# In the first three pairs POOL makes one of the eight broadcast additions of the attention scores

## What is computed

```python
x = emb[tokens] * jnp.sqrt(jnp.float32(D_MODEL))
x = x + positional_encoding(N, D_MODEL)[None, :, :]
q = x @ Wq + bq
k = x @ Wk + bk
v = x @ Wv + bv
scores = jnp.einsum('d,bijd->bij', attn_scale, jnp.tanh(q[:, :, None, :] + k[:, None, :, :]))
weights = jax.nn.softmax(scores, axis=-1)
attn = jnp.einsum('bij,bjd->bid', weights, v)
attn = attn @ Wo + bo
x = layer_norm(x + attn, g1, beta1)
h = jax.nn.relu(x @ W1 + bf1)
y = h @ W2 + bf2
return layer_norm(x + y, g2, beta2)
```

## Time and profile before

| | us |
|---|---|
| median of 3 runs | 890.82 |
| lowest and highest | 890.13, 891.63 |
| the profiled execution | 891.35 |
| its span, first to last instruction | 889.5 |
| busy, of the span: PE, DVE, ACT, POOL | 788.0, 659.6, 656.9, 324.7 |
| mean granted clock of TensorE (share of full) | 0.956 |

### The profile page before, as it was taken

How to read it: one execution, slowest core, us unless ns; L and a number is a source line. 1 busy time by engine, 2 the same in 40 slices (tenths; PEclk the granted TensorE clock), 3 DMA queues, 4 the chain that set the end, 5 groups by cost and what they waited for, 6 DMA issues and landing times. The chain is left out here.

```text
span 889.5 us, 22649 instructions
## 1 busy us (share of the span) xinstructions
PE 788.0 (89%) x7286; PEld 607.1 (68%) x7286; DVE 659.6 (74%) x2165; ACT 656.9 (74%) x1498; POOL 324.7 (36%) x397
## 2 busy tenths in 40 slices
PE   0857998998989989899899999987889999999798
PEld 0534665765766656667656666664779999999687
DVE  2997899999999999999999999553423344443675
ACT  1775999999898988998999999765335565655444
POOL 3110124334343353343433523444414545555121
PEclk9978999999999999999999999997889999999899
DMA  8129889889899889898898898894089999995411
GB/s 163 49 55 210 189 191 208 193 188 212 188 204 206 183 180 206 181 204 187 182 210 176 187 206 181 196 208 102 21 279 387 376 395 403 324 360 191 149 30 36
DMA packets 82305, 177.77 MB, mean 200 GB/s; under 512 B 8244, under 2 KB 35339, under 8 KB 82240
## 3 DMA queue, kind: packets, MB, share of 16 engines
q1 hardware_dynamic: 65536, 164.01, 73.9%
q0 software_dynamic: 5760, 7.92, 2.7%
q10 hardware_dynamic: 10944, 5.02, 2.1%
HBM read 65.93 MB, written 113.34 MB: 202 GB/s over the span
## 5 line engine op out<-in xcount | busy, mean ns | idle before, releaser
L879 DVE TENSOR_TENSOR arena<-qT,b_qk 128x2304 f32<-128x2304 f32 x128 | 323.8, 2543 | 1.6 <-DVE v_bias L904 0.3
L615 ACT ACTIVATE arena<-arena 128x2304 f32<-128x2304 f32 x128 | 271.6, 2122 | 41.8 <-DVE arena L879 40.9
L1324 PE MATMUL b_s<-arena,apad 128*32 128x192 f32 x3072 | 160.4, 345 | 30.9 <-ACT p L624 24.2
L760 ACT ACTIVATE act_h<-big,arena 128x128 f32<-128x128 f32 x336 | 96.1, 369 | 74.1 <-PE big L1641 69.7
L1324 PEld LDWEIGHTS b_s<-arena,apad 128*32 128x32 f32 x3072 | 90.5, 113 | 87.8 <-issue 43.0
L541 POOL TENSOR_TENSOR kept<-kept,rs 96x384 f32<-96x384 f32 x64 | 52.7, 824 | 215.0 <-DVE rs L1026 214.8
L589 POOL DMA_INDIRECT eo_dram<-gT,toff x84 | 82.5, 983 | 96.3 <-issue 64.3
L658 ACT ACTIVATE kept<-kept,mx 96x96 f32<-96x96 f32 x256 | 92.3, 365 | 11.9 <-DVE mx L1019 11.3
L1641 PE MATMUL big<-hbT,arena 128*128 128x128 f32 x672 | 91.2, 280 | 2.3 <-DVE hbT L1207 1.2
L1641 PEld LDWEIGHTS big<-hbT,arena 128*128 128x128 f32 x672 | 83.6, 196 | 3.1 <-issue 2.1
L1207 DVE TENSOR_SCALAR hbT<-b_t,cols 128x128 f32<-128x128 f32 x84 | 34.4, 409 | 65.0 <-PE b_t L1634 65.0
(11 more groups left out here) (209 smaller groups left out, 1441.4 us busy)
## 6 DMA issues: line engine op xcount, KB each, us to landing
rows_dram<-act_h SPq DMA_DIRECT2D x32, 3096.0 KB
arena<-in_wpack SPq DMA_DIRECT2D x84, 578.0 KB
prT<-rows_dram ACTq DMA_DIRECT2D x76, 64.5 KB
arena<-eo_dram SPq DMA_DIRECT2D x4, 512.0 KB, 6.9
x_dram<-res SPq DMA_DIRECT2D x16, 96.0 KB
out<-of SPq DMA_DIRECT2D x12, 128.0 KB, 1.8
eo_dram<-gT,toff POOLq DMA_INDIRECT x84
rows_dram<-rows_now,slot_now POOLq DMA_INDIRECT x64
```

The lines of the kernel that those rows point to most:

```text
L615: act.activation(v, v, ACT.Tanh).then_inc(s["tanh"], 1)
L760: last = act.activation(act_h[:, i, c * TILE:(c + 1) * TILE], big[i][:, c * TILE:(c + 1) * TILE], ACT.Silu, bias=wslot[:, slot, 2 * DFF + ...
L879: dve.tensor_tensor(ring[c % TRING].rearrange("p (x m n) -> p x m n", m=CQ, n=N), qv.unsqueeze(3).to_broadcast([D, SPLIT * QG, CQ, N]), kv ...
L1324: last = pe.matmul(b_s[32 * a:32 * a + 32, 0:SPLIT * N], apad[:, 31 - line:63 - line], t[:, :, a, m, :], start=(line == 0), stop=(line == ...
```

## The change

A helper `adds(p, c)` counts VectorE's additions up to chunk c of pair p, since the first three pairs have seven of them. In pairs 0, 1 and 2 (HELPED = 3) `qk_evac` first copies the keys from PSUM to a new SBUF tile kT; chunk 4 (HELD) is left out of VectorE's list and is made by POOL in `help_add`, from kT, which stands in POOL's list between root h0 and normalise 3. `help_add` waits for the queries of the pair and for score 0 of it. ScalarE's tanh 4 waits for POOL's semaphore `add_pool`. The waits on the semaphore `add` are counted anew. From pair 3 on, the list of instructions is as before, except for one wait on `add_pool` in pair 3.

```diff
@@ -52,6 +52,7 @@
 CH = G * CPB
 CW = SPLIT * QG * CQ * N
 TRING = 4
+HELPED, HELD = 3, 4
 EARLY = 2
 DEPTH = 5
 VC = D + 2
@@ -64,6 +65,13 @@
 WCOLS = 2 * DFF + FC + D
 
 ROWS = ["bo", "g2", "beta2", "bs2", "fbf2"]
+
+
+def adds(p, c):
+
+    if known(p) and p < HELPED:
+        return p * (CH - 1) + c - (c > HELD)
+    return p * CH + (c - HELPED)
 
 
 def known(value):
@@ -183,6 +191,7 @@
         xs = sb("xs", [N, G, D])
         xT = sb("xT", [D, TN])
         qT = sb("qT", [D, TN])
+        kT = sb("kT", [D, TN])
         bqk = sb("bqk", [D, 1])
         vrow = sb("vrow", [N, G, VC])
         nmax = sb("nmax", [128, SPLIT])
@@ -280,7 +289,7 @@
 
         s = {n: ctx.enter_context(nc.semaphore("s_" + n)) for n in [
             "ids", "ld_a", "ld_b", "late", "consts", "gate", "pool_c", "setup_mm", "setup",
-            "raw_mm", "raw_ev", "emb0", "emb1", "emb2", "eid", "xs", "kept", "xs_t", "xT", "qk", "qk_ev", "add", "tanh", "score",
+            "raw_mm", "raw_ev", "emb0", "emb1", "emb2", "eid", "xs", "kept", "xs_t", "xT", "qk", "qk_ev", "add", "add_pool", "tanh", "score",
             "nmax", "exp1", "p1t", "p1T", "vp", "vp_ev", "att", "x1", "x1h", "x1_t", "x1T", "x1bT", "f", "f_ev", "y2",
             "x2", "h0_rows", "xa", "xa_t", "xaT", "hg", "hg_ev", "hv", "hv_ev", "s2", "s2_ev", "exp2", "rs2", "pn",
             "t2", "t2_ev", "o_init", "o", "res", "tn", "tn_t", "hT", "r", "rT", "lg", "routed",
@@ -298,6 +307,15 @@
         BANK_G = [big[0], big[1], big[2], big[0]]
         BANK_V = [big[1], big[2], big[0], big[1]]
         block = ctx.enter_context(nc.Block())
+
+        def add_chunk(eng, c, keys):
+            g, cc = c // CPB, c % CPB
+            qv = qT[:, g * N:(g + 1) * N].rearrange("p (x m) -> p x m", m=QM)[:, :, CQ * cc:CQ * cc + CQ]
+            kv = keys[:, g * N:(g + 1) * N]
+            return eng.tensor_tensor(
+                ring[c % TRING].rearrange("p (x m n) -> p x m n", m=CQ, n=N),
+                qv.unsqueeze(3).to_broadcast([D, SPLIT * QG, CQ, N]),
+                kv.unsqueeze(1).unsqueeze(1).to_broadcast([D, SPLIT * QG, CQ, N]), ALU.add)
 
         def gate(eng, sem, value):
 
@@ -526,6 +544,13 @@
                     gate(pool, s["eid"], p - (EARLY - 1))
                 gather_rows(emb[:, g, :], eidx_now[:, g:g + 1], s["emb2"])
 
+            def help_add(p):
+                if not (known(p) and p < HELPED):
+                    return
+                pool.wait_ge(s["qk_ev"], p + 1)
+                pool.wait_ge(s["score"], p * CH + HELD - TRING + 1)
+                add_chunk(pool, HELD, kT).then_inc(s["add_pool"], 1)
+
             def root(p, n):
                 pool.wait_ge(s["var_" + n], p + 1)
                 pool.tensor_tensor(rstd[n][:, :], ve[n][:, :], halves[:, 0:G], ALU.pow)\
@@ -565,6 +590,7 @@
                 at(n, 2, root, "x2")
                 at(n, 3, normalise, 2)
                 at(n, 2, root, "h0")
+                at(n, 0, help_add)
                 at(n, 3, normalise, 3)
                 at(n, 5, scatter_rows, 1)
                 at(n, 4, keep_rows)
@@ -610,7 +636,10 @@
             act.preload_act_table(ACT.Exp)
 
             def tanh(p, c):
-                act.wait_ge(s["add"], p * CH + c + 1)
+                if known(p) and p < HELPED and c == HELD:
+                    act.wait_ge(s["add_pool"], p + 1)
+                else:
+                    act.wait_ge(s["add"], adds(p, c) + 1)
                 v = ring[c % TRING]
                 act.activation(v, v, ACT.Tanh).then_inc(s["tanh"], 1)
 
@@ -867,20 +896,19 @@
 
             def qk_evac(p):
                 dve.wait_ge(s["qk"], p + 1)
-                wait(dve, s["add"], p * CH)
+                wait(dve, s["add"], adds(p, 0))
+                if known(p) and p <= HELPED:
+                    wait(dve, s["add_pool"], p)
+                if known(p) and p < HELPED:
+                    dve.tensor_copy(kT[:, :], p_k)
                 dve.tensor_scalar(qT[:, :], b_qk[:, 0:TN], bqk[:, :], None, ALU.add).then_inc(s["qk_ev"], 1)
                 dve.wait_ge(s["qk_ev"], p + 1)
 
             def add(p, c):
+                if known(p) and p < HELPED and c == HELD:
+                    return
                 wait(dve, s["score"], p * CH + c - TRING + 1)
-                g, cc = c // CPB, c % CPB
-                qv = qT[:, g * N:(g + 1) * N].rearrange("p (x m) -> p x m", m=QM)[:, :, CQ * cc:CQ * cc + CQ]
-                kv = p_k[:, g * N:(g + 1) * N]
-                dve.tensor_tensor(
-                    ring[c % TRING].rearrange("p (x m n) -> p x m n", m=CQ, n=N),
-                    qv.unsqueeze(3).to_broadcast([D, SPLIT * QG, CQ, N]),
-                    kv.unsqueeze(1).unsqueeze(1).to_broadcast([D, SPLIT * QG, CQ, N]), ALU.add)\
-                    .then_inc(s["add"], 1)
+                add_chunk(dve, c, p_k).then_inc(s["add"], 1)
 
             def x_rows(p):
                 early = known(p) and p < EARLY
@@ -1333,7 +1361,7 @@
 
             def qk(p):
                 pe.wait_ge(s["xT"], p + 1)
-                wait(pe, s["add"], p * CH)
+                wait(pe, s["add"], adds(p, 0))
                 for i in range(2):
                     last = pe.matmul(b_qk[:, i * TN:(i + 1) * TN], wqk[:, i, :], xT[:, :], start=True, stop=True)
                 last.then_inc(s["qk"], 1)
```

## The result

| | before | changed |
|---|---|---|
| median of 13 runs each, us | 890.14 | 894.29 |
| lowest and highest | 887.09, 892.72 | 891.09, 899.87 |
| ratio, with its 95% interval | | 1.0057, 1.0037 to 1.0076 |
| the profiled execution, and its span | 891.35, 889.5 | 894.29, 892.4 |
| busy, of the span: PE, DVE, ACT, POOL | 788.0, 659.6, 656.9, 324.7 | 784.2, 659.0, 656.7, 336.6 |

The changed kernel is slower, by 0.0057 x 890.14 = 5.1 us (3.3 to 6.8); the two medians lie 4.15 us apart. The forecast of 896.1 lay 1.8 us above the measured median, inside its range. But two of its terms were wrong, one in each direction, and so the total alone would teach the wrong thing.

The account below looks back on a forecast made before the run. The prediction took the first three turns to be bound by one pair's chain and the later loop by three busy engines; (d - 2.31) - 0.39 + (d - 1.88) gave +5.3 us, median 896.1, range 893.0 to 900.0.

Parts of the forecast that it names:

- The frame: Whole loop: three busy arithmetic engines, paced by pairs not fills; a shift at the third turn reaches the end in full.
- The price d: POOL's addition of 2304 columns, each helped pair: 4.95 us, from L541 in proportion, with bounds 2.28 and 6.54.
- 2d - 4.58: Sum of the delays of pairs 0, 1 and 2, with d POOL's addition time: +5.3 us for d = 4.95.
- d - 2.58: Pair 0: how much later TensorE's `products` begin behind POOL's late chunk; +2.37 us forecast.
- S1: Lateness of pair 1's first addition: 2.37 for `products` plus 0.27 for the copy of keys, 2.64 us.
- rival C: Pair 2: the hole before xa_turn brings a longer slow-clock stretch on TensorE, costing 1.7 us; 897.8, chance 0.06.
- Pair 1: Second helped turn: gain of 0.66 us at x1T, less 0.27 for the copy of keys, so -0.39.
- d - 1.88: Pair 2: delay added because xa_norm is held until POOL's addition ends; total lateness there 5.34 us.
- Rival A: Pair 2: xa_norm isn't held by POOL's addition, total lateness there 3.4 us; 894.2, chance 0.12.
- The copy of the keys: Pairs 0, 1 and 2: VectorE's added PSUM to SBUF copy ahead of qT, 3 x 0.27 us.
- Rival B: Helped pairs: POOL needs 2.84 ns a column, 6.54 us per addition, +10.1 us in sum; 900.9, chance 0.10.
- D: Helped pairs: POOL's addition is over when VectorE's would have been, making the kernel faster; 886.6, chance 0.04.

Follow-up runs that it names:

- help2: Changed kernel with POOL's addition, the copy and the left-out addition in pair 2 alone; one run 891.49 us beside 891.41 for before.
- early0_bs2: early0 with VectorE's bs2q moved out of `setup` to behind it; 884.16 us over 12 runs against 888.77 for before, ratio 0.9951.
- warm_turns: Kernel before with 52 idle matmuls in TensorE's waits of turns 1 and 2; 884.27 us over 8 runs, ratio 0.9955 to before.
- early0_warm: early0_bs2 with 52 idle matmuls in TensorE's waits of turns 1 and 2; 881.44 us over 6 runs, ratio 0.9912 to before.
- xa_first: Changed kernel with POOL's addition of pair 2 waiting until xa_norm has run; 889.44 us in one run, then timed 889.32 us, ratio 1.0001 to before.
- help0: Changed kernel with pair 0 alone helped (HELPED = 1); one run 893.33 us beside 891.41 for before.
- warm_after: Changed kernel with 24 idle matmuls on TensorE in turn 0, around xs_turn and ahead of `products`; one run 894.74 us beside 894.83.
- early0: Kernel with pair 0 alone helped, POOL's addition placed ahead of keep_x(0), not waiting for `setup`; one run 889.74 us beside 894.83.

## Why the prediction was right, and where it was not

**The frame held.** What bounds the loop, that the delay at the third turn is carried on, and that the fills don't set the pace: SP again waited for `res` in 13 waits, 371.2 us in total (368.9 before), and help2 excludes the fills directly. Inside the loop "in full" held too: of the 6.55 us at pair 3, 5.13 reach pair 15, but nearly half of the difference is the long turn in before's profile, and the 0.09 us a turn go with the three helped pairs and not with being late (help2 loses nothing up to pair 8). Behind the loop it is shown less well. The medians of four timed kernels differ from before's by about what their loops were shifted (changed +4.15 for +5.13, early0_bs2 -4.6 for -4.2, warm_turns -4.5 for -4.9, early0_warm -7.3 for -5.8); xa_first's differs by +0.55 for +4.24.

**The price d: the term was mis-sized.** 4.95 forecast, 4.04 measured, inside the bounds of 2.28 and 6.54. The row of L541 in proportion was chosen for its broadcast operand. In proportion takes it that nothing of a short row is a fixed part, though 256 columns took 727 ns and 384 only 824; so it gives too much. Measured at 2304 columns it is 1.75 ns a column. By the forecast's own formula, 2d - 4.58, the sum would have been 3.5 us, not 5.3. The Trainium skill, GPSIMD Engine Reference, section 3.1 (Elementwise — side-by-side cycle accounting), gives 4497 ns for 2048 columns, an estimate of 5.06 us here. The trace does not agree with it, 4.04, and the measurement decides.

**Pair 0: the wait was right, a term was missing.** POOL's start (29.27, forecast 29.54), the chain tanh 4, tanh 5, v_copy, `products`, and x_rows held until POOL ends: all seen. With d = 4.04 the formula d - 2.58 gives +1.46 for `products`, measured +1.34. The step of the prediction that failed is "They now begin at 38.93: +2.37 ... S1 = 2.64", which takes it that `products` last as long as before. In the changed kernel, and in help0, they ran at half the clock: +2.50 us until score 5, so S1 was 4.11. warm_after shows it, by keeping the clock up (one profile). The forecast had the clock as rival C, in another place (pair 2), at 1.7 us, with a chance of 0.06. It was no side case here: low clock from 30 to 102 us grew from 27.3 to 37.5 us.

**Pair 1: the gain did not come.** Forecast -0.39, measured +0.21. tanh 4 at 61.34 lay only 0.78 behind 56.45 + 4.11. But rsum, forecast to gain 0.68, came at 60.89, 0.45 later than 56.33 + 4.11, since attend1 ran in the low stretch (1.18 against 0.69) behind a score 1 that did too. No run isolates this, but the profiles agree: attend1 took 0.69 in xa_first and warm_after, which gained 0.90 and 0.57 in this pair, and 1.18 in xa_first_timed, which lost 0.16. "Late next here are attend1 and ScalarE's chain, both" was right in what it named and took TensorE's durations from before.

**Pair 2: right.** xa_norm is held until POOL's end + 0.34, and tanh 4 is released by ScalarE's own xaT, not by POOL. With the measured d, d - 1.88 = 2.16; measured 2.24. help2 shows it alone, xa_first takes it away. Rival A, that xa_norm isn't held, fell. The lock as the Trainium skill, SBUF — State Buffer, section Who interferes with whom, has it agrees in every form met here. Held until POOL ended: xa_norm (4.32 us for 0.59), x_rows (2.53 for 0.41), bs2q (1.45 for 0.22). Not held: the additions with one SBUF input (in early0 two in 5.01 us from 22.83, the second wholly inside POOL's).

**The copy of the keys:** forecast 0.81 in all, measured 0.56 at pair 3 and, up to pair 8, no less.

**So two errors offset.** 2 x 0.91 = 1.8 us too much for d; some 3 us too little for the clock (2.50 in pair 0, about 0.6 in pair 1), and from that 1.4 came off by pair 15, nearly half of it in before's own profile. That +5.3 met +5.1 (or 4.15 by the medians) was luck. Rival B (d = 6.54) fell by d itself, D (d below 2.3) too; what D wanted, a helper that is done in time, came about in early0 not by a shorter addition but by an earlier one. The forecast had costed the place behind keep_x(0), yet not asked what the other place would be worth: 5.7 us at pair 1 (+3.78 against -1.89).

**What stays open.** Why a turn of the loop is 0.09 us shorter with three pairs helped; why the low stretches of the expert stage fall as they do, which makes single profiles differ by several us; why xa_first has the time of before although its loop ends 4.2 us late in the timed profile; and whether an addition of pair 1 or 2 in a better place would gain, which wasn't tried.

## What to carry to other kernels

When a helper engine takes a piece of a start-up chain, its place in the helper's queue and what it locks out weigh more than its speed: the same 4.04 us addition cost 3.8 us behind a wait for `setup` (2.2 to 2.5 of it by the lower clock) and gained 1.9 ahead of it. Where an engine waits several microseconds in a turn, don't carry its durations over from the old profile: read the granted clock of the stretch behind each hole, and give "TensorE works at half the clock after the hole" a term of its own in the sum. And for a size that the trace doesn't show, short rows bound from both sides: their slope gave 2.28 us, in proportion they gave 4.95 and 6.54, and 4.04 lay between; "in proportion" is better kept as an upper bound than taken as the value.

## What the runs showed of the hardware

- POOL adds 128x2304 fp32 with both operands broadcast from SBUF in 4.04 us (4.04 to 4.05 in every run), 1.59 times VectorE's 2.54 with keys in PSUM.
- VectorE's xa_norm and bs2q (tensor_scalar within SBUF) and x_rows (two SBUF inputs), when they meet a running POOL addition, aren't slowed but stopped: they end 0.08 us (bs2q), 0.28 us (x_rows) or 0.34 us (the two halves of xa_norm) behind POOL's end, however long they were held. VectorE's addition, one input in PSUM, runs through beside it in 2.54 to 2.56 us.
- Filling TensorE's waits in turns 1 and 2 with matmuls whose result nobody uses left 0.0 us (warm_turns) and 3.4 us (early0_warm) at the low clock from 30 to 102 us, and this alone made the kernel before 0.9955 times as long (4.5 us of the medians). The 22 ahead of score 0 of turn 1 lay in a wait: with them, score 0 started no later (48.15 against 48.31).
